# Graph layer on one core: most tiles of the second and third stream written as two plain blocks

## What is computed

```python
h = relu(layernorm(x))
for l in range(2):
    m = relu(h[src] + xe)
    mean[r, n] = sum of m over edges of type r into node n, divided by their number
    h = einsum('rnd,rdo->no', mean, weight[l]) + h @ root[l] + bias[l]
    h = batch_norm(h) ; relu after the first layer
out = x + h
```

## Time and profile before

| | us |
|---|---|
| median of 3 runs | 2361.72 |
| lowest, highest | 2359.91, 2362.99 |
| the profiled execution | 2347.37 |
| its span | 2345.3 |

### The profile page before, as it was taken

The page is one execution under the profiler, slowest core; times in us unless marked ns, Lnnn a source line. Parts: engine busy times, 40 slices in busy tenths (PEclk is TensorE's granted clock), DMA queues, the critical chain, the costliest instruction groups (busy, mean ns, idle before and its releaser), DMA issues. The chain is left out here.

```text
span 2345.3 us, 58410 instructions
## 1 busy us (share of the span) xinstructions
PE 1950.2 (83%) x22268; PEld 1623.0 (69%) x22268; DVE 1434.1 (61%) x4328; ACT 1193.5 (51%) x2472; POOL 1443.9 (62%) x1377
## 2 busy tenths in 40 slices
PE   2499999999998889799788887787778787769866
PEld 1288888888777767799676675666556566659855
DVE  8766777777776565488765554444444444528554
ACT  0166777877776665344244443343333343424565
POOL 6746777777777775200377777777777777741000
PEclk8599999999999999899898999988998889979966
DMA  8724555555554553799633333333323333259799
GB/s 325 304 83 130 148 158 162 157 153 157 148 152 137 155 159 92 283 418 417 222 111 110 110 107 96 97 93 98 89 83 97 88 99 90 68 198 329 243 416 402
DMA packets 260695, 409.54 MB, mean 175 GB/s; under 512 B 38627, under 2 KB 170334, under 8 KB 260412
## 3 DMA queue, kind: packets, MB, share of 16 engines
q1 hardware_dynamic: 192566, 225.92, 29.2%
q0 software_dynamic: 46192, 99.84, 14.7%
q10 hardware_dynamic: 21654, 79.99, 8.4%
HBM read 255.41 MB, written 150.19 MB: 173 GB/s over the span
## 5 line engine op out<-in xcount | busy, mean ns | idle before, releaser
L853 POOL DMA_INDIRECT acc<-arena x550 | 583.9, 1062 | 223.6 <-issue 160.6
L1775 PE MATMUL ps_o<-arena 128*128 128x128 f32 x3152 | 458.9, 306 | 217.8 <-DVE arena L1224 215.2
L1775 PEld LDWEIGHTS ps_o<-arena 128*128 128x128 f32 x3152 | 420.8, 215 | 305.6 <-DVE arena L1224 298.5
L838 POOL DMA_INDIRECT arena<-h_rows,arena x394 | 438.9, 1114 | 301.0 <-DMA h_rows<-chunk_mem 181.2
L838 POOL DMA_INDIRECT arena<-in_x_dram,arena x394 | 403.4, 1024 | 125.5 <-issue 119.7
L1706 PE MATMUL ps_t<-arena 128*128 128x256 f32 x1576 | 453.2, 411 | 12.1 <-DVE arena L1198 8.1
L1198 DVE TENSOR_SCALAR arena<-arena 128x256 f32<-128x256 f32 x788 | 273.9, 410 | 128.3 <-PE ps_o L1725 128.1
L1184 DVE TENSOR_TENSOR arena<-arena,bn_b 128x512 f32<-128x512 f32 (+1 forms) x99 | 69.7, 704 | 448.7 <-DMA arena<-h_rows,arena 448.7
L1706 PEld LDWEIGHTS ps_t<-arena 128*128 128x128 f32 x1576 | 274.7, 194 | 96.2 <-issue 69.5
L1511 ACT ACTIVATE arena<-ps_o 1x512 f32<-1x512 f32 (+1 forms) x196 | 113.2, 577 | 423.7 <-PE ps_o L1775 423.6
L1480 ACT ACTIVATE arena<-ps_t 128x512 f32<-128x512 f32 x396 | 233.2, 589 | 179.7 <-PE ps_t L1706 179.5
(11 more groups left out here) (281 smaller groups left out, 2399.8 us busy)
## 6 DMA issues: line engine op xcount, KB each, us to landing
arena<-in_edge_attr_dram SPq DMA_DIRECT2D x190, 256.0 KB
chunk_mem<-acc SPq DMA_DIRECT2D x55, 512.0 KB, 8.4
acc<-arena ACTq DMA_DIRECT2D x28, 896.0 KB, 24.0
arena<-in_x_dram SPq DMA_DIRECT2D x45, 512.0 KB, 9.7
arena<-acc SPq DMA_DIRECT2D x43, 512.0 KB, 12.4
chunk_mem<-hn_rows SPq DMA_DIRECT2D x41, 512.0 KB, 12.7
out_dram<-arena ACTq DMA_DIRECT2D x38, 512.0 KB, 9.0
acc<-arena SPq DMA_DIRECT2D x238, 56.0 KB
```

The source lines that it names most:

```text
L838: pool.indirect_dma_start(out=hb[:, hb_slot(gg), t // NG, :], out_offset=None, in_=(x, h1_tab)[l], in_offset=at(src_t[:, t:t + 1])).then_i ...
L853: pool.indirect_dma_start(out=acc[l], out_offset=at(idx_t[:, t:t + 1]), in_=ob[:, gg % OB, t // NG, :], in_offset=None, **how).then_inc(co ...
L1775: last = te.matmul(ps_sum[:, c], sm[:, gg % SM, b, j, :], yb[:, gg % 2, b, j, :], start=b == 0, stop=b == NH - 1)
```

## The change

- The spans of tiles that go out as plain blocks grow: tiles 1 to 95 stay at 112 rows in one block; 100 to 130 are written with 127 rows in one block; 131 to 194 and 199 to 285 with 255 rows in two blocks, 127 and 128 rows. That makes 277 tiles in each layer, 151 of them with two blocks; 117 tiles are left to the scatter.
- A tile with two blocks has a second node matrix (places less 128) and two more matmuls in `node_sums`. Their result stands in the bank `product_bank(gg, 1)`; ACT copies it to `ob` ahead of the main copy. `products` of half 1 now waits for `ob_ready`, not `yb1_ready`, before it writes that bank.
- `ob` gets 6 columns and three buffers instead of four; SP writes windows 7 steps behind instead of 10.
- The places are computed from a bf16 view of `pm` (the upper halves of its words), against two bf16 columns per tile (value and remainder); DVE adds the two.
- DVE's setup computes widths for four spans over three blocks of 128 tiles instead of two spans over one.

```diff
-    HB, XB, SM, OB = 20, 4, 2, 4
+    HB, XB, SM, OB = 20, 4, 2, 3
-    MT, LAG = 3, 10
+    MT, LAG = 3, 7
-    WROWS = 112
-    SPANS = ((1, NG - 4), (NG + 1, NG + 24))
+    SPANS = ((1, NG - 4, 112, 1), (NG + 1, NG + 31, 127, 1), (NG + 32, 2 * NG - 4, 255, 2), (2 * NG + 1, 2 * NG + 87, 255, 2))
+    WROWS = {t: rows for a, b, rows, n in SPANS for t in range(a, b + 1)}
+    def further(g):
+        return [t // NG for t in tiles(g) if t in WROWS and WROWS[t] >= P]
...
+                    if t - 1 not in WIDE:
+                        sp.wait_ge(scat_out[(gg - 1) % OB], 16 * tiles_done(gg - 1, OB))
                     first = sp.value_load(first_i[0:1, t:t + 1], min_val=0, max_val=P * (F + WB * P - 1))
-                    sp.dma_start(acc[l][bass.ds(first, WROWS), :], ob[1:1 + WROWS, gg % OB, t // NG, :]).then_inc(wide_out, 16)
+                    rows = min(WROWS[t], T)
+                    sp.dma_start(acc[l][bass.ds(first, rows), :], ob[1:1 + rows, gg % OB, t // NG, :]).then_inc(wide_out, 16)
+                    if t // NG in further(g):
+                        k = H + further(g).index(t // NG)
+                        sp.dma_start(acc[l][bass.ds(first + T, P), :], ob[:, gg % OB, k, :]).then_inc(wide_out, 16)
...
+                    own.link(v.tensor_copy(place_mid[:, :, 0:w], at[:, :, 0:w, 1]))
+                    own.link(v.scalar_tensor_tensor(place_i[:, :, 0:w], at[:, :, 0:w, 0], 0.25, place_mid[:, :, 0:w], ALU.add, ALU.add))
                     dve.sem_inc(rounded, 1)
-                    own.link(v.tensor_copy(place_at[:, g, :, 0:w], place_i[:, :, 0:w]))
+                    own.mark(v.tensor_copy(place_at[:, g, :, 0:w], place_i[:, :, 0:w]))
+                    more = further(g)
+                    if more:
+                        own.mark(v.tensor_scalar(place_at[:, g, :, H:H + len(more)], place_i[:, :, more[0]:more[-1] + 1],
+                                                 -float(P), None, ALU.add))
+                    own.join()
...
+                    w += len(further(g))
                     for b in range(NH):
                         ins = v.tensor_tensor(sm[:, gg % SM, b, 0:w, :], iota_f[:, 0:P].unsqueeze(1).to_broadcast([P, w, P]),
...
+                n = len(further(g))
+                if n > 0:
+                    a_.activation(ob[:, gg % OB, H:H + n, :].rearrange("p w d -> p (w d)"), product_bank(gg, 1)[:, 0:n * D], ACT.Copy)
...
-                    last = te.matmul(ps_side[:, k:k + 1], pm[:, g % 2, j, b * P:(b + 1) * P], ikey_t[:, t:t + 1], start=True, stop=True)
+                    top = pm[:, g % 2, j, b * P:(b + 1) * P].bitcast(BF16)[:, 1:2 * P:2]
+                    last = te.matmul(ps_side[:, 2 * k:2 * k + 2], top, place_b[:, t, :], start=True, stop=True)
...
-                    wait(pe, (yb_ready, yb1_ready)[b], gg - 1)
+                    wait(pe, (yb_ready, ob_ready)[b], gg - 1)
...
+                    if sorted_:
+                        for k, j in enumerate(further(g)):
+                            for b in range(NH):
+                                last = te.matmul(product_bank(gg, 1)[:, k * D:(k + 1) * D], sm[:, gg % SM, b, H + k, :], yb[:, gg % 2, b, j, :],
+                                                 start=b == 0, stop=b == NH - 1)
```

More of the change, by code:

```diff
@@ L120, in tiles @@
         return [s * NG + g for s in range(H) if s * NG + g < NT]
-    WROWS = 112
-    SPANS = ((1, NG - 4), (NG + 1, NG + 24))
-    WIDE = [t for a, b in SPANS for t in range(a, b + 1)]
+    SPANS = ((1, NG - 4, 112, 1), (NG + 1, NG + 31, 127, 1), (NG + 32, 2 * NG - 4, 255, 2), (2 * NG + 1, 2 * NG + 87, 255, 2))
+    WIDE = [t for a, b, rows, n in SPANS for t in range(a, b + 1)]
+    WROWS = {t: rows for a, b, rows, n in SPANS for t in range(a, b + 1)}
     WB = WIDE[-1] // P + 1
-    assert all(a % NG > 0 and b % NG + 2 < NG and a // NG == b // NG for a, b in SPANS) and WROWS < P
+    FURTHER = 2
+    assert all(a % NG > 0 and b % NG + 2 < NG and a // NG == b // NG and rows < n * P for a, b, rows, n in SPANS)
+    def further(g):
+        return [t // NG for t in tiles(g) if t in WROWS and WROWS[t] >= P]
     def listed(g):
@@ L136, in windows @@
     def windows(gg):
-        return sum(len(in_window(k % NG)) for k in range(gg + 1))
+        return sum(len(in_window(k % NG)) + len(further(k % NG)) for k in range(gg + 1))
+    assert all(len(further(g)) <= FURTHER and (not further(g) or len(tiles(g)) == H) for g in range(NG))
+    assert all(further(g) == list(range(further(g)[0], further(g)[-1] + 1)) for g in range(NG) if further(g))
     ORDER = [(g, t) for g in range(NG) for t in tiles(g)]
@@ L987, in _ @@
             own.link(v.memset(behind[:, :], 1.0))
-            for a, b in SPANS:
+            for a, b, rows, n in SPANS:
                 own.link(v.scalar_tensor_tensor(behind[:, :], t0, float(SPARE_ROW + P * (b + 1)), behind[:, :],
@@ L1042, in _ @@
             dve.wait_ge(flag_ps, 1)
-            for k, (a, b) in enumerate(SPANS):
+            for k, (a, b, rows, n) in enumerate(SPANS):
                 end = (b // NG + 1) * NG
                 own.link(v.tensor_tensor(near_end[:, k:k + 1], dst_t[0:1, end:end + 1], dst_t[0:1, b:b + 1], ALU.subtract))
-                own.link(v.tensor_scalar(near_end[:, k:k + 1], near_end[:, k:k + 1], float(WROWS), None, ALU.is_lt))
+                own.link(v.tensor_scalar(near_end[:, k:k + 1], near_end[:, k:k + 1], float(rows), None, ALU.is_lt))
             own.link(v.tensor_copy(most[0:1, :], ps_s[0][0:1, 0:1]))
@@ L1052, in _ @@
             spares = srcf[0:1, :, :].rearrange("p b e -> p (b e)")[:, 0:WB * P]
-            own.mark(v.tensor_scalar(spares, iota_f[0:1, 0:WB * P], float(P), float(SPARE_ROW), ALU.mult, ALU.add))
+            for b in range(WB):
+                own.mark(v.tensor_scalar(spares[:, b * P:(b + 1) * P], iota_f[0:1, 0:P], float(P), float(SPARE_ROW + b * P * P), ALU.mult, ALU.add))
             own.join()
@@ L1132, in counts_in @@
                     dve.wait_ge(inv_ps, 5)
-                    own.link(v.tensor_copy(inv_t[:, :], ps_side[:, :]))
+                    own.link(v.tensor_copy(inv_t[:, :], ps_side[:, 0:NTA]))
                     own.link(v.memset(inv_t[0:1, :], 1.0))
@@ L1751, in products_any @@
                     wait(pe, yb_ready, gg - 1)
-                    wait(pe, yb1_ready, gg - 1)
+                    wait(pe, ob_ready, gg - 1)
                     for j, t in enumerate(tiles(g)):
```

52 lines of the change are left out of this document (32 added, 20 removed).

## The result

| | before | after |
|---|---|---|
| median of 4 runs each, us | 2360.81 | 2755.41 |
| lowest to highest | 2357.21 to 2362.99 | 2751.16 to 2757.86 |
| ratio after / before | | 1.1671, 95% interval 1.1652 to 1.169 |
| the profiled execution, its span | 2347.37, 2345.3 | 2754.17, 2752.4 |

A forecast was written before the change was run, and what follows sets the result against it. Bound: landing of two serial 127-row blocks in one DMA engine, 12.0 us per step. Layer 0 +325, layer 1 +241, setup +8, tail -14: +561 on 2347.4, plus 14.3: 2922 us; own range 2730 to 3260, widened to 2530 to 3260.

The forecast's parts named there:

- 127 rows go through one DMA engine: SP's plain blocks: 127 has no divisor to deal rows out by, so one engine carries each block; forecast's chance 0.80.
- The price of 3.47 us per block, and both in the same engine: Block DMAs: 127 packets at 27.3 ns take 3.47 us; a step's two blocks queue in one engine, 6.9 us.
- The fixed part: Block DMAs, issue to landing: 2.5 us latency, plus about 0.6 us for other work in that engine.
- Groups 1 to 31: Groups with one two-block tile fewer than groups 32 to 87, given the same 12.0 us per step in both layers.
- the window loop: Both layers: a group's windows wait until all those of the group before have landed; 12.0 us per step, groups 1 to 87.
- the half-chunk loop: Layer 0: SP waits for `ob_ready` before loading the half chunk that DVE needs; 11.4 us per step, not the bound.
- SP held at the issue: SP's queue: each 127-row issue might hold SP for 3.91 us, as in the setup; 339 us more.
- the upper bound: Slow end of the forecast's range: steps of 13.95 us with SP held at 127-row issues, 3260 us.
- Setup +8 and tail -14: DVE's longer setup adds 8 us before the first step; POOL's tail from last `sums_out` to join halves, 14 us less.
- The clock: PE: idling 40% of a step, it may be granted 1.2 GHz for part of it; the granted clock would fall.
- The first rival: 127-row blocks are spread over the engines like 112-row ones: 9.2 us steps in layer 0, -75, 2287 us; chance 0.13.
- The bf16 places: PE's 8 place matmuls, 1.95 us a step in layer 0, become bf16; 0.6 us taken as left.

The follow-up runs named there:

- the pair with one block: The changed kernel with one stream's 127-row block cut to 126 rows: 2537.8 us with the 127-row block in the third stream, 2386.3 with it in the second.
- the fastest kernel: The changed kernel with blocks of 112 and 128 rows (240 in all) and windows 10 steps behind again: 2109.5 us, ratio to before 0.9008.

## Why the prediction was right, point by point

- *127 rows go through one DMA engine.* Right, though taken from a single, crowded spot of the setup. It is now shown by the pair of kernels that differ in one row, 2755 and 2314 us, and by the packets: while the blocks are on their way 7.3% of 16 engines are busy with 127 rows, one engine, and 12.7% with 122, two. By the Trainium skill, page "DMA: Bandwidth & Descriptors", section "Why a DMA increments its semaphore by 16 and not by 1", a copy is dealt over the largest number of engines up to 16 that divides its slowest dimension; 126 has 14, 122 has 2, 127 has 1. The trace agrees for 127 (7.3% busy) and 122 (12.7%), and the times agree that 126 and 122 are cheap (2314 and 2312 us); that 126 rows use 14 engines no row here shows. No row names the engine either.
- *The price of 3.47 us per block, and both in the same engine.* Right within 0.15 us as the price of a second block: 5.22 us for one block alone, 8.54 for two, a difference of 3.32. The packets themselves follow each other faster than the 27.3 ns of the earlier trace rows, every 22.8 ns (57 in 1.3 us), which would be 2.9 us for 127 of them. That both queue in one engine is shown by the packets and fits the pair with one block.
- *The fixed part.* Mis-sized, and this is the term that was wrong for layer 1. From the first 127-row issue to the landing of both blocks I added 2.5 us of latency, read from the indirect join of three rows, 6.9 us of data and 0.6 us for what else goes through that engine, 10.0 us. Measured are 8.54 in the group shown. With data at 27.3 ns a packet, 1.6 to 1.75 us are left for both other terms instead of 3.1; at the 22.8 ns seen in the trace it would be 2.7, and part of the error is in the data. How it splits was not measured. So the step of 12.0 us was 1.3 us too long in layer 1 (10.71): 72 us over groups 32 to 87. With the 1.73 us of groups 1 to 31 (12.0 less 10.27), 54 us, it makes up the 127 us between +241 forecast and +114 measured.
- *Groups 1 to 31.* I gave them the same 12.0 as the rest, because they too have two 127-row blocks. Measured are 11.09 and 10.27, each less than in groups 32 to 87. They have one 128-row block instead of two and less work on PE and DVE; what of that makes the 0.4 us of layer 1 was not tried.
- *Which loop binds layer 0.* The order was wrong. I put the window loop at 12.0 and the half-chunk loop at 11.4. Measured are 10.7 and 12.03. The first was too long, as said; the second too short by 0.6, and I did not count that SP is held at the 128-row issues (0.67 and 2.09 us in the median of groups 32 to 87, instead of 0.35 each) ahead of the half chunk, nor what that chunk waits in the same engine. That the forecast of 12.0 us was hit in layer 0 (12.03) is luck: the time is that of the other loop. So is much of how close the sum came there (+294 measured, +325 forecast).
- *SP held at the issue.* I placed it at the 127-row issue and only in the upper bound (3.91 us). It happens, but at the issue behind it, with a median of 2.04 us, and only behind the second slow block is it long. Most of it lies within the wait for the landing and costs layer 1 nothing.
- *Setup +8 and tail -14.* Neither is there. The first `sums_out` starts 3.8 us earlier, so DVE's longer setup was covered. In layer 0 the join's DMA is issued 15.5 us after the last `sums_out`, 12.9 before: the last three groups are scattered by POOL in both kernels, and after the last `sums_out` ten scatters were still to come, eight before.
- *The clock.* Granted 0.84 in layer 0 and 0.92 in layer 1, with PE busy 73 and 79%. It was low where PE had gaps, as forecast. In layer 1 of the kernel with 126 rows it was back at 0.99, and in the fastest kernel at 1.00.
- *The first rival*, spread blocks, is what the kernel with 126 rows is: 2314.5 against the 2287 worked out for it, or -31 us against -75, as the kernel before took 2345 beside it. Its layer 1 step (7.8) was hit, its layer 0 step (9.2) was measured at 10.1.
- *The bf16 places.* I took 0.6 of 1.95 us a step as left, 1.35 less. Where they are on the path the step is 1.41 us shorter. What they give in this kernel was not measured; as forecast, the blocks' loops lie above.

All in all the mechanism of layer 1 was the forecast one, with the landing of the blocks mis-sized; that of layer 0 was the second loop, which the prediction had, but put behind the first. The forecast was 167 us too high: 127 from layer 1 and 31 from layer 0, 12 from the setup, 13 because the profiled execution of after lies only 1 us below its median where that of before lay 14 below, less 17 for the tails (the terms are rounded).

## What to carry to other kernels

Choose the rows of a plain DMA by their divisors before their number: 112 and 128 rows are cheap here where 127 of the same 512 bytes took 5.2 us to land, and one row less was worth 441 us. Then write down each loop that a semaphore closes through a DMA's landing (first issue, issues in between, last landing, register load), and the queue's own round of issues, and compare both with the engines' step: two further issues a step were free in layer 1 (7.87 us against 7.79), where the round stayed near that step, and cost 0.8 us in layer 0, where it passed it. The share of busy DMA engines in a stretch with one transfer alone tells how many engines carry it. And a good change can be hidden by a bad part in it: the same edit with other block sizes and the old lag is 9.9% faster than the kernel before.

## What the runs showed of the hardware

- The row count of a plain block decides how many engines carry it: 127 rows of 512 bytes keep one engine busy (7.3% of 16, a packet every 22.8 ns), 122 rows two (12.7%, every 13.7 ns). From issue to landing one 127-row block took 5.22 us and two behind one another 8.54; the indirect join of three rows takes 2.5 us.
- Behind two such blocks the next issue on the same queue is held, 2.25 us in the median (layer 1, groups 32 to 87); behind one it takes 0.66 to 0.72, and 0.35 otherwise. The 127-row DMA itself is issued in 0.27 us, quicker than one of 112 rows (0.34).
- Place in the queue matters as much as size: with a single slow block per group the kernel took 44 us more than before when it was issued 1.2 us after its group's first, and 196 us more when issued 3.1 us after it (2386.3 and 2537.8 against 2342).
